# Modulation rows loaded onto all partitions, multiplies on GpSimd, and two tails of block 0 side by side

## The reference, cut to what matters

```python
ctx   = causal_ema(x, tau_ctx)
gated = x * sigmoid([x, ctx] @ Wg.T + bg)
h1    = gelu(x @ Wn1.T + bn1)
mod   = 0.5 + sigmoid(h1 @ Wn2.T + bn2)                  # (b, t, 16)
traces[d]  = causal_ema(gated * mod[..., d:d+1], tau_raws[d])   # 16 depths
temporal   = sum over d of traces[d] * softmax(blend)[d]
gate  = sigmoid(temporal @ Wtemp.T + btemp)
soma  = gelu(x @ Wsoma.T + bsoma)
out   = (soma * gate) @ Wout.T
L0    = (out - mean(out)) / sqrt(var(out) + 1e-5) * gamma + beta
```

## Time and profile before

| | |
|---|---|
| median of 3 runs | 2878.78 us (2876.46 to 2880.01) |
| the profiled execution's own time | 2876.17 us |
| its span in the trace | 2874.4 us, mean granted clock 0.993 |
| PE / DVE / ACT / POOL busy | 98% / 64% / 48% / 43% |
| first step's first matmul | at 125.70 us |

### The profile page before, as it was taken

The page is one execution under the profiler, slowest core; times in us unless marked ns, Lnnn a source line. Parts: engine busy times, 40 slices in busy tenths (PEclk is TensorE's granted clock), DMA queues, the critical chain, the costliest instruction groups (busy, mean ns, idle before and its releaser), DMA issues.

```text
span 2874.4 us, 36550 instructions
## 1 busy us (share of the span) xinstructions
PE 2818.4 (98%) x13018; PEld 2331.4 (81%) x13018; DVE 1846.4 (64%) x3017; ACT 1390.2 (48%) x2408; POOL 1233.3 (43%) x950
## 2 busy tenths in 40 slices
PE   8699999999999999999999999999999999999999
PEld 5488888788888888888788888888888888888888
DVE  8699778867777766556865666655776563333443
ACT  4544555465336633454534553344643473333445
POOL 5256434643463445433554345542455333333333
PEclk9899999999999999999999999999999999999999
DMA  4133332322112311111311131111221122111231
GB/s 150 60 116 99 90 94 78 111 92 93 57 48 68 115 48 50 48 50 48 94 45 48 56 92 45 48 45 52 74 70 57 47 87 63 50 45 44 72 92 57
DMA packets 85573, 201.22 MB, mean 70 GB/s; under 512 B 10312, under 2 KB 27152, under 8 KB 85392
## 3 DMA queue, kind: packets, MB, share of 16 engines
q1 hardware_dynamic: 82256, 190.38, 21.5%
q0 software_dynamic: 2560, 8.39, 1.0%
q10 hardware_dynamic: 576, 0.11, 0.0%
HBM read 190.75 MB, written 8.09 MB: 69 GB/s over the span
## 4 chain that ended last, share of the span: by engine, by line
PE 88%; DVE 7%; issue 2%; ACT 2%; DMA 1%; SPq 0%; DVEq 0%; ACTq 0%
PE bank L557 19%; PE bank L559 19%; PE bank L558 19%; PE ps_out L557 9%; PE ps_out L559 9%; PE ps_out L558 9%; DVE trace L1075 2%; DVE w_lo L1145 2%; DVE trace L1067 1%; PE bank L550 1%; PE bank L631 1%; DVE hid L1169 0%; DMA stat<-mod_rows 0%; ACT L867 0%; PE bank L679 0%
## 5 line engine op out<-in xcount | busy, mean ns | idle before, releaser
L1308 POOL TENSOR_TENSOR hid_lo<-hid,hid_hi 128x512 fp32r<-128x512 f32 x640 | 865.6, 1353 | 1581.2 <-ACT hid_hi L954 1580.9
L557 PE MATMUL bank<-res_lo,w_hi 128*128 128x512 f32 x2432 | 963.3, 396 | 6.2 <-DVE res_lo L1160 3.3
L559 PE MATMUL bank<-res_hi,w_hi 128*128 128x512 f32 x2432 | 953.1, 392 | 0.0
L558 PE MATMUL bank<-res_hi,w_lo 128*128 128x512 f32 x2432 | 951.9, 391 | 0.0
L1169 DVE TENSOR_TENSOR hid<-hid,bank 128x512 f32<-128x512 f32 x576 | 393.3, 683 | 540.8 <-PE bank L559 512.8
L926 ACT ACTIVATE hid<-bank 128x512 f32<-128x512 f32 x576 | 344.0, 597 | 663.9 <-PE bank L559 662.8
L1145 DVE TENSOR_TENSOR w_lo<-w_raw,w_hi 128x768 fp32r<-128x768 f32 (+2 forms) x520 | 513.5, 989 | 177.9 <-ACT w_hi L895 139.6
L895 ACT ACTIVATE w_hi<-w_raw 128x768 fp32r<-128x768 f32 x392 | 331.4, 845 | 540.0 <-PE ps_out L559 513.4
L559 PEld LDWEIGHTS bank<-res_hi,w_hi 128*128 128x128 f32 x2432 | 458.3, 188 | 103.3
L557 PEld LDWEIGHTS bank<-res_lo,w_hi 128*128 128x128 f32 x2432 | 458.8, 189 | 100.5 <-issue 6.7
L558 PEld LDWEIGHTS bank<-res_hi,w_lo 128*128 128x128 f32 x2432 | 459.3, 189 | 86.4
(11 more groups left out here) (179 smaller groups left out, 1624.4 us busy)
## 6 DMA issues: line engine op xcount, KB each, us to landing
w_raw<-in_chunks SPq DMA_DIRECT2D x392, 384.0 KB
w_raw<-in_head_chunks SPq DMA_DIRECT2D x64, 224.0 KB
x_in<-in_xT SPq DMA_DIRECT2D x16, 256.0 KB, 3.6
pre_x<-in_xT SPq DMA_DIRECT2D x14, 256.0 KB, 7.0
soma_rows<-pre_soma SPq DMA_DIRECT2D x14, 256.0 KB, 2.0
soma<-soma_rows SPq DMA_DIRECT2D x14, 256.0 KB, 3.1
out_yT<-acc SPq DMA_DIRECT2D x7, 512.0 KB, 2.8
acc<-in_sidew SPq DMA_DIRECT2D x2, 512.0 KB, 7.1
```

Of the source, the lines that this page charges most:

```text
L557: mm(out, wh, xl, start=start and i == 0, stop=False, skip_group_check=not lone)
L558: mm(out, wl, xh, start=False, stop=False, skip_group_check=not lone)
L559: last = mm(out, wh, xh, start=False, stop=end, skip_group_check=not lone)
L1308: nc.gpsimd.tensor_tensor(hid_lo[i % DEPTH][:], hid[i % 3][:], f(hid_hi[i % DEPTH][:]), ALU.subtract).then_inc(s_hlo, 1)
```

## The change

For blocks 1 to 7, the selection matmul, the DVE multiply and the three small DVE operations of piece 5 are gone. Instead:

- `pre` makes 0.5+0.5*tanh on POOL before it is stored; `mod_rows` is stored as one row of 16 x 256.
- SP loads rows 0 and 1 of it onto all 128 partitions (into `temporal`); ACT's queue loads the other fourteen, two per DMA (`spread`): four DMAs after the gate of piece 5, into `one_hi, one_lo, two_hi, two_lo`, and three more after `weigh` 7, 9 and 11.
- ACT makes `gated * bl[d]` (`weigh`, a Copy with a per-partition scale, two halves) two pieces before the scan, POOL multiplies by the row (`mul`) one piece before, DVE only scans, POOL adds. Four trace buffers in a ring (`ema` is the fourth).
- `side_cost` of a depth piece rises from 2.1 to 2.5 for these blocks, that of piece 5 falls to 0.

In block 0 the order of pieces from 23 on is new: lane 0's pieces 23 to 32 come between lane 1's scans, then from piece 33 on both lanes take turns. The early weight cuts, `part0` and the table preloads move from lane 0's pieces to lane 1's.

```diff
 def side_cost(b, j):
     if 7 <= j < 7 + ND:
-        return 2.1
+        return 2.5 if b else 2.1
...
-    for j in range(12, PIECES):
+    for j in range(12, 23):
         turns0 += [(0, j), (1, j - 5)]
-    turns0 += [(1, j) for j in range(PIECES - 5, PIECES)]
+    turns0 += [(0, 23), (0, 24), (0, 25), (0, 26), (1, 18), (0, 27), (1, 19), (0, 28), (0, 29), (0, 30), (1, 20), (0, 31),
+               (0, 32), (1, 21)] + [(1, j) for j in range(22, 33)]
+    for j in range(33, PIECES):
+        turns0 += [(0, j), (1, j)]
...
-        if s == 0 and j in EARLY:
+        if s == 1 and j in EARLY:
             out += [("cut", EARLY[j]), ("cut_lo", EARLY[j])]
...
+FROM_DRAM = {
+    "act": [f"weigh{d}" for d in range(ND)],
+    "pool": ["mul0", "mul1", "mul2"] + [x for d in range(2, ND + 1) for x in [f"add{d - 1}"] + [f"mul{d + 1}"] * (d + 1 < ND)],
+}
...
+        mod_on = [[t[s][:].bitcast(fp32) for t in (one_hi, one_lo, two_hi, two_lo)] for s in range(BB)]
+        ring = [trace[s] + [ema[s]] for s in range(BB)]
...
 # SP, pre_back
-                sp.dma_start(stat[s][0:ND, :], mod_rows[u]).then_inc(s_back[s], 16)
+                sp.dma_start(temporal[s][:].rearrange("p h t -> p (h t)"),
+                             mod_rows[u, 0:2 * S].partition_broadcast(P)).then_inc(s_on[s][4], 16)
...
 # PE
-                if ahead and j in (2, 3, 4):
+                if ahead and (j in (2, 3, 4) or 7 <= j < 7 + ND):
                     return
...
 # ACT
+            def spread(b, s, i):
+                u = (b - 1) * BB + s
+                act.wait_ge(s_store[u % 3], 32 * (u // 3 + 1))
+                act.dma_start(mod_on[s][(i - 1) % 4].rearrange("p h t -> p (h t)"),
+                              mod_rows[u, 2 * i * S:2 * (i + 1) * S].partition_broadcast(P)).then_inc(s_on[s][(i - 1) % 4], 16)
+
+            def weigh(b, s, d):
+                if d >= ND:
+                    return
+                if d == 0:
+                    act.wait_ge(l_dve[s], dve_at(s, b, "gated"))
+                elif d == 4:
+                    act.wait_ge(l_dve[s], dve_at(s, b, "scan0"))
+                elif d > 4:
+                    act.wait_ge(l_pool[s], pool_at(s, b, f"add{d - 4}"))
+                for h in range(DH):
+                    last = activate(ring[s][d % 4][:, h, :], gated[s][:, h, :], ACT.Copy, scale=bl[:, h, d:d + 1])
+                last.then_inc(l_act[s], 1)
+                if d in (7, 9, 11):
+                    spread(b, s, (d + 3) // 2)
...
-                    if lead:
+                    if b == 0 and s == 1:
                         activate(junk[:, 0:1], eps[:], ACT.Sqrt)
...
 # DVE, depth piece of blocks 1 to 7
+                        dve.wait_ge(l_pool[s], pool_at(s, b, f"mul{max(d, 1)}"))
+                        for h in range(DH):
+                            last = V.tensor_tensor_scan((temporal[s] if d == 0 else tr)[:, h, :],
+                                                        ps[:, S + d:S + d + 1].broadcast_to([P, S]),
+                                                        tr[:, h, :], 0.0, ALU.mult, ALU.add)
...
 # POOL
+                if b and 6 <= j < 6 + ND:
+                    d = j - 6
+                    i = d // 2
+                    pool.wait_ge(l_act[s], act_at(s, b, f"weigh{d}"))
+                    if d == 0:
+                        pool.wait_ge(s_on[s][4], 16 * b)
+                    elif d % 2 == 0:
+                        k = (i - 1) % 4
+                        pool.wait_ge(s_on[s][k], 16 * ((2 if k < 3 else 1) * (b - 1) + (i - 1) // 4 + 1))
+                    row = (mod_on[s][(i - 1) % 4] if i else temporal[s][:]).rearrange("p h t -> p (h t)")[:, d % 2 * S:(d % 2 + 1) * S]
+                    nc.gpsimd.tensor_tensor(ring[s][d % 4][:], ring[s][d % 4][:], row.unsqueeze(1).broadcast_to([P, DH, S]),
+                                            ALU.mult).then_inc(l_pool[s], 1)
```

More of the change, by code:

```diff
@@ L83, in side_cost @@
     if 7 <= j < 7 + ND:
-        return 2.1
+        return 2.5 if b else 2.1
     if b == 0 and j in (1, 26, 30, 32, 45):
         return 0.0
-    return {0: 1.3, 5: 1.0, 34: 1.7, 36: 1.4, 42: 1.5, 24: 0.0, 25: 0.0, 29: 0.0, 37: 0.0, 43: 0.0}.get(j, 0.7)
+    return {0: 1.3, 5: 1.0 if b == 0 else 0.0, 34: 1.7, 36: 1.4, 42: 1.5, 24: 0.0, 25: 0.0, 29: 0.0, 37: 0.0, 43: 0.0}.get(j, 0.7)
 def step_budget(i):
@@ L120, in order @@
             out.append(("setup", "bias"))
-        if s == 0 and j == 40:
+        if s == 1 and j == 40:
             out.append(("setup", "part0"))
-        if s == 0 and j in EARLY:
+        if s == 1 and j in EARLY:
             out += [("cut", EARLY[j]), ("cut_lo", EARLY[j])]
@@ L254 @@
 SIDE_POOL = [f"add{d}" for d in range(1, ND)]
+FROM_DRAM = {
+    "act": [f"weigh{d}" for d in range(ND)],
+    "pool": ["mul0", "mul1", "mul2"] + [x for d in range(2, ND + 1) for x in [f"add{d - 1}"] + [f"mul{d + 1}"] * (d + 1 < ND)],
+}
 SPLITS = {"x_hi", "ctx_hi", "t_hi", "p_hi", "q_hi", "x_lo", "ctx_lo", "t_lo", "p_lo", "q_lo", "xT_lo", "probT_lo"}
 def stages_in(stages, s, b):
-    if 1 <= b <= PRE and stages is not SIDE_DVE:
-        return [x for x in stages if x not in ("h1", "soma", "mod")]
+    if 1 <= b <= PRE:
+        if stages is SIDE_POOL:
+            return FROM_DRAM["pool"]
+        gone = ("h1", "soma", "mod", "mod_hi", "modpair")
+        left = [x for x in stages if x not in gone and not x.startswith("mix" if stages is SIDE_PE else "mul")]
+        if stages is SIDE_ACT:
+            k = left.index("alpha") + 1
+            left[k:k] = FROM_DRAM["act"]
+        return left
     if b:
@@ L414, in residual_stack_kernel @@
         s_back = [sem(f"pre_back{s}") for s in range(BB)]
+        s_on = [[sem(f"mod_in{s}_{i}") for i in range(5)] for s in range(BB)]
         s_y = [sem(f"y_out{i}") for i in range(NACC)]
@@ L835, in side @@
                     last.then_inc(l_act[s], 1)
+                    if b:
+                        for i in range(1, 5):
+                            spread(b, s, i)
                     if b == 0:
@@ L841, in side @@
                     activate(lead_alpha[:, 0:ND] if lead else ps[:, S:S + ND], alpha[:, 0:ND], ACT.Copy).then_inc(l_act[s], 1)
+                elif 6 <= j < 7 + ND and b:
+                    for d in (0, 1) if j == 6 else (j - 5,):
+                        weigh(b, s, d)
                 elif j == 25 and b:
@@ L1043, in side @@
                 elif j == 5:
-                    if 1 <= b <= PRE:
-                        dve.wait_ge(s_back[s], 32 * b)
-                    else:
-                        dve.wait_ge(l_act[s], act_at(s, b, "mod"))
+                    if b:
+                        return
+                    dve.wait_ge(l_act[s], act_at(s, b, "mod"))
                     TS(mod, mod, 0.5, 1.0, ALU.mult, ALU.add).then_inc(l_dve[s], 1)
@@ L1057, in side @@
                     d = j - 7
-                    tr = trace[s][d % 3]
+                    tr = ring[s][d % 4] if b else trace[s][d % 3]
+                    if b:
+                        if d == 0:
+                            dve.wait_ge(l_act[s], act_at(s, b, "alpha"))
+                        dve.wait_ge(l_pool[s], pool_at(s, b, f"mul{max(d, 1)}"))
[3 more added lines that the diff above has]
+                                                        tr[:, h, :], 0.0, ALU.mult, ALU.add)
+                        last.then_inc(l_dve[s], 1)
+                        return
                     if d == 0:
@@ L1071, in side @@
                     if d == 0:
-                        dve.wait_ge(l_act[s if b else 0], act_at(s if b else 0, b, "alpha"))
-                    decay = ps[:, S + d:S + d + 1] if b else lead_alpha[:, d:d + 1]
+                        dve.wait_ge(l_act[0], act_at(0, b, "alpha"))
+                    decay = lead_alpha[:, d:d + 1]
                     for h in range(DH):
@@ L1082, in side @@
                     dve.wait_ge(l_act[s], act_at(s, b, "tgate"))
+                    if b:
+                        dve.wait_ge(s_back[s], 16 * b)
                     STT(trace[s][0][:], trace[s][0][:], 1.0, soma[s][:], ALU.add, ALU.mult).then_inc(l_dve[s], 1)
@@ L1302, in side, with pre @@
                         pool.wait_ge(l_pool[s], pool_at(s, b, f"add{d - 1}"))
-                    nc.gpsimd.tensor_tensor(temporal[s][:], temporal[s][:], trace[s][d % 3][:],
+                    nc.gpsimd.tensor_tensor(temporal[s][:], temporal[s][:], (ring[s][d % 4] if b else trace[s][d % 3])[:],
                                             ALU.add).then_inc(l_pool[s], 1)
+                if b and 6 <= j < 6 + ND:
+                    d = j - 6
+                    i = d // 2
+                    pool.wait_ge(l_act[s], act_at(s, b, f"weigh{d}"))
+                    if d == 0:
+                        pool.wait_ge(s_on[s][4], 16 * b)
[5 more added lines that the diff above has]
+                                            ALU.mult).then_inc(l_pool[s], 1)
+            def pre(u, k):
+                if k == 3:
```

(4 more changed lines are left out.)

10 lines of the change are left out of this document (5 added, 5 removed).

## The result

The changed kernel takes 2899.3 us (median of four runs, 2897.0 to 2901.1) against 2877.6 for the kernel before, run beside it: ratio 1.0074, interval 1.0062 to 1.0086. It is 21.7 us slower; 2847 was forecast.

The account below looks back on a forecast made before the run. PE, 98% busy, was taken as the bound after 126 us of block 0's side work. 2876.2 - 40.3 - 3.9 + 10 + 2 = 2844.0, median 2.6 above: 2847 us; forecast range 2834 to 2860, 8 in 10 2826 to 2879.

Parts of the forecast that it names:

- part 4: Depth work: POOL and DVE take turns; POOL's multiply hidden except in head steps of blocks 0, 2, 4; +10 us.
- rival of lock-outs: Head stretch: w_lo waits behind gapless POOL work, up to 6.9 us an event; 2862 us or more, chance 0.17.
- in dozens: Sign that the prediction is wrong: w_lo's of over 5 us coming in dozens.
- Part 1: PE's stream: 224 selection matmuls removed at 0.18 us each, 40.3 us off; lower bound 24.6.
- Part 2: Piece 5: DVE's wait for the modulation load goes, with PE's wait for x1 and clock loss; 3.9 us off.
- Part 3: Depth multiplies moved to ACT and POOL: added work hidden, each hand-over asked one piece ahead, some 10 us.
- Part 5: Block 0's tail in its new order: first step at 126 to 129 us, +2 us; bounds -4 and +6.
- Part 6: Row loads of 256 KB per lane: 2.7 us to landing each, hidden; bounds 0 and 2 us x 14.
- PE's wait sum after the lead passes 60 us: Sign that the prediction is wrong, read from PE's waits after the first 126 us.
- the waits would move to hid_lo: Expected sign: PE's waits move from DVE's trace to hid_lo around the first head steps, near 500 us.

Follow-up runs that it names:

- e18: The changed kernel with the side_cost numbers of before and POOL's multiply cut to 4 of 512 columns, waits kept; 2844.5 us.
- e11: The changed kernel with the two side_cost numbers of before; 2879.0 us.
- e3: The changed kernel with POOL's multiply cut to 4 of 512 columns, all waits kept; 2858.7 us.
- e17: The changed kernel with the side_cost numbers and block 0's tail order of before, leaving the changed depth work alone; 2874.0 us.
- e1_no_mix: The kernel before without the selection matmuls of blocks 1 to 7, DVE multiplying by whatever the bank holds; 2840.2 us.
- e4: The changed kernel without any row load, POOL multiplying by a row of x already there; 2884.6 us.
- e10_resident_mul0: The changed kernel without row loads (POOL multiplies by a row of x) and with the first scan waiting for multiply 0 only; 2881.8 us.
- e2_tails_only: The kernel before with only the new order of block 0's pieces, its early cuts and table preloads; 2881.4 us.
- e7: The changed kernel with rows 0 and 1 loaded earlier, at piece 0 of the lane; 2888.9 us.
- e14: The changed kernel with DVE instead of POOL multiplying, one operation per tile, weigh kept, rows 0 and 1 loaded earlier, side_cost of before; 2865.9 us.
- e19: The changed kernel with LAG, the offset between the two lanes in the list, at 11 instead of 12; 2858.0 us.

## Why the prediction was wrong

The matmuls are gone and worth nearly what was said. The kernel was to be 32 us faster and is 21.7 slower, for which the prediction had a chance of 0.12. Two steps failed: the multiply was priced 24.6 us too low, and the new order, 20.3 us, wasn't priced.

**The step that failed first: part 4, the multiply on POOL, +10.** It was taken as hidden but for three head stretches. In the old list it costs 34.6 us (e18 against e11), in the changed one 40.7 (e3). The depth work alone, with the old order, gains 3.2 us (e17) where parts 1, 2 and 4 gave 34.2. So the forecast would have missed without the new costs too: with them undone the kernel takes 2879.0 us (e11). In the LAG 11 list the multiply wasn't cut by itself.

The rival of lock-outs was on the list, with a chance of 0.17. The lock-outs came longer, not "in dozens": 8 groups, 59.5 us in sum. The argument against that rival was that "POOL soon runs out of work when DVE's scans stop"; at 517 it had 13 instructions without needing one scan more, hid_lo, adds and multiplies of earlier scans. The rival's own price was too low as well: at 6.9 us an event, five more give the 2882 that it names for ten. How much of the 34.6 us is lock-out, and how much is POOL's queue, no run separates. The multiply took 1.29 to 1.68 us by tile, 1.55 on the mean, for 1.38 forecast.

**The step that was missing: the costs.** The prediction used the new `side_cost` only to count depth pieces (29 in the first 40 steps, part 4) and gave the new order no price and no rival. It costs 17.0 us in the kernel before and 20.3 in the changed one. The list could have been counted ahead: one step between x1 and scores in 14 of 14 lanes against 5 stood in it. The earlier trace rows had the price of such a place, 2.12 us of waiting for x1, with a clock loss beside it. The count would have warned, not forecast the 20 us.

**Part 1, the matmuls, -40.3:** 36.5 by e1_no_mix. Right in kind; 3.8 too much.

**Part 2, piece 5, -3.9:** wrong in place and in sign. The wait for the DMA went off DVE, but DVE now waits for POOL: 7.41 us at 962.71, behind a transfer again, where 3.92 us stood. Over all lanes DVE waits 36.3 us in 13 lanes for the first multiplies; before it was 36.9 for the transfer itself. Behind most of the new waits stands `weigh`, not the transfer, and without any transfer 30.8 us are left (e4). "The first row has a piece more to arrive" counted program order as time.

**Part 3, "each is asked for one piece ahead":** true from depth 2 on, false for depth 0. The first scan waits for multiply 1, which POOL starts in the scan's own piece. With the load gone and only this undone, DVE's waits there all but vanish, but only 2.8 us come back (e10_resident_mul0), hardly clear of noise. ACT's load is hidden, as said: weigh takes 0.496 us for 0.470 forecast.

**Part 5, tails, +2:** +4.8 by e2_tails_only, inside the bounds of -4 and +6. The first step was forecast at 126 to 129 us and came at 131.35.

**Part 6, DMA, hidden:** half right. The loads cost 14.7 us in the changed list (e4), 10.4 of it by rows 0 and 1 (e7), and nothing measurable in the old one with POOL's multiply cut (e18). At the worst place the first multiply started 6.4 us after the issue at 952.5, not 2.7. And 2.7 was misread: the earlier trace rows mixes the stores of `soma_rows` (2.0 us to landing) with its loads, which landed after 3.1 us before the change.

**The tells:** "PE's wait sum after the lead passes 60 us" came true, 67.6. It was written for POOL's queue, and both causes are in it: with the old costs PE stands still for 49.5 us (e11), with the multiply cut for 36.3 (e3). That the waits would move to hid_lo did not come true: it has 7.4 us of them.

**What the parts give together:** -36.5 (matmuls) + 4.8 (tails) + 34.6 (multiply) + 20.3 (costs, in the changed kernel, with what the loads and the late multiplies add in that list) = +23.2, for 21.7 measured. The last two terms are differences along the same row of runs (e18, e11, the changed kernel), so what this sum tests is only that e18 lies where the first two put it, 31.7 us below before: it is 32.7 below.

**Open:** why the multiply on DVE still costs some 26 us (e14 at 2865.9 against e1 at 2840.2, same list, same tails), though DVE is at 65% of the span there and only 46 us busier (1875.3 against 1829.7). Its second operand now comes from SBUF, where it came from PSUM; that this is the reason is argued from part 4's row, not shown. In the old list the multiply with its row in SBUF takes back most of the 36.5 us of the matmuls, on DVE (26) as on POOL (34.6). Nor was the kernel before run with another LAG. Its own list with LAG 11 also has one step between 36 and 38 in a single lane, so how much of e19's gain is a good list, and not the change, isn't known.

## What to carry to other kernels

A constant that feeds a scheduler is an edit of the program order: write both lists and count the distances between dependent pieces before the sum is made; a count far from the old one is a warning. Price a moved operation with its new operands and its new neighbours, and not by its duration alone: here 224 multiplies of some 1.5 us, on an engine that is busy for 54% of the span, cost 35 us. When several engines walk one list in order, a new hand-over puts the latest of them ahead of everybody's next work; look for what stands right behind the first use in each queue. When a change that should pay loses, move the offset of the schedule by one notch before giving up the idea: here it was worth twice the loss. Move it in the kernel before as well, which was not done here.

## What was unexpected of the hardware

- A DVE operation with two SBUF inputs can wait through a whole run of back-to-back POOL instructions: 15.95 us behind 13 of them, 15.54 in e19_lag11, where at 208 us one got in after the first. It isn't only w_lo: a scan with both inputs in SBUF took 3.47 us for two (170.03 us), where its mean is 0.82 each. Scans with one input in the bank had a mean of 0.67 us and took 0.69 at most (L1116).
- A wait of PE brings a loss of clock with it, here 0.3 to 0.4 of its length: 67.6 us of standing still came with 26.1 us of clock loss, 26.7 with 7.3 before. Around the 7.71 us wait the granted clock was 0.66 from 960 to 970 us, 3.4 us of the loss, and 1.00 again from 970. Of these 3.4 us 1.5 fall into the wait itself.
- A broadcast load of 256 KB to 128 partitions lands 3.4 to 5.0 us after its issue by the medians of its five targets, against 3.1 for the plain load of `soma` before; that load, next to the broadcasts, rose to 3.4.
